# The reciprocals of a bidirectional scan moved from VectorE to ScalarE's Ln and Exp, in a fused attention and FFN kernel

## The chip, the cores and the metric

One core of one Trainium2 chip. The metric is the device time of one launch in microseconds. The kernel before was run three times: 1677.47 us is the median (1675.44 to 1679.04).

## The reference

Four sequences (NB = 4) of 512 positions and 512 channels pass through one block. `f` is a second input of the same shape; both scans use it as their `k` and as their `v`.

```python
# _bi_wkv, per channel; called twice, with other w and u
tf    = sigmoid(sum(time_emb))                      # one number per sequence
decay = exp(-exp(w)) * (0.5 + 0.5 * tf)
ek, ekv = exp(min(k, 30)), exp(min(k, 30)) * v
nf, df = scan(a = a * decay + ekv, b = b * decay + ek)            # forward
nb, db = the same scans from the end
euk = exp(min(u + k, 30))
num = nf + nb - ekv + euk * v
den = df + db - ek + euk
out = sigmoid(r) * (num / max(den, 1e-8)) * (0.8 + 0.2 * tf)

x = x + attention(bi_wkv(x, f, f, w1, u1))   # 16 heads of 128, segments of 128 with a memory (delta rule), then Wo
x = x + ffn(bi_wkv(x, f, f, w2, u2))         # silu(x W1) * (x W3), Walsh-Hadamard transform over 2048, then W2
```

## The kernel before

Everything is written by hand for five queues: `tensor` (TensorE), `vector` (VectorE, DVE in the profile), `scalar` (ScalarE, ACT), `gpsimd` (GpSimd, POOL) and `sync` (SyncE, SP, most DMAs). Each queue runs its instructions in order and waits on semaphores, so an instruction that waits holds up all that stands behind it on its engine. Matrix products are made of three products of split numbers (a high part and what is left): of each weight, ScalarE writes the high part (`split_hi`, L1246, tile `wh`) and GpSimd the rest (`split_w`, L1619, tile `wl`).

**The scans.** The work of `_bi_wkv` is cut into 32 tiles of 128 channels x 512 positions, 16 for each scan. `scan(t, name)` in `vector` writes one step of tile `t`: `df`, `nf` the forward scans (denominator, numerator), `db`, `nb` the backward ones, `mn` and `mu` the minima for the next tile, `d2`, `n2` the sums, `d3` the clamp and the sigmoid of r (L874), `rc0` to `rc3` four reciprocals of 128 columns each (L880), `oy` the output (L885). ScalarE makes the exponentials (`exp_k`, `exp_u`, `exp_r`) and `yh`, GpSimd the products `EKV`, `EUV` and `yl`; `yh` and `yl` are what TensorE needs of a tile.

**The head.** Tiles 0 to 3 come first, with nothing beside them. TensorE's `chunk(c)` makes the first head group's k, v and q from tile `c`: k and v and q take 12 products of 512 columns and 12 of 256. It starts when `yh`, `yl` of tile `c` and the three weights are there. Tiles 0 and 2 use one set of buffers, 1 and 3 another. Behind tile 2, VectorE also makes the mixing weights from `betas` (L1107 to L1111); SP then stores them (`beta_s`), and ScalarE's queue loads them with `load_ombeta(0)`, `load_beta(0)`, which wait for the store and stand ahead of `high_y(3)`.

**The grid.** 32 groups of two heads follow (`n` = 0 to 31). In each, every engine passes eight slots, `behind(n, k)`. A planner, `shared_out()`, deals the steps of tiles 4 to 23, then of the transform of W2 and of z, over the slots: each slot has room in ns (`ROOM`, `BURST_ROOM`), each step a cost in VectorE's time (`SCAN`; 0 for steps of other engines), and the order is that of the table. All engines use the same table, so a step of ScalarE stands in the slot in which its place in the table falls. Where a slot stands on ScalarE: 1 ahead of the copy of the next group's first half of v (`copy_v(nx, 0)`), 4 ahead of the first copy of k, 6 ahead of the first copy of q, 7 behind it and ahead of the second copy of q. Every fourth group is a burst (`n` = 4, 8, ...): TensorE then also does the output projection `wo` and all of k and q at the group's end.

**The FFN.** 32 steps (`u`) follow; tiles 24 to 31 are dealt over them by `shared_out_ffn()`. The first steps wait for weights of the first two hidden blocks, "1", "3" and "2" of blocks 0 and 1.

Of the kernel before, what the change touches and what calls it, by code (L numbers as in the profile page):

```python
# [44 lines left out]
def seg(s):  # L45
# [22 lines left out]
for _i in range(8):  # L68
    for name, cost in HADAMARD:
        if name != "mult":  # L70
            STEPS.append((name, _i, cost))
        elif _i > 0:
            if _i == 2:
                STEPS += [(z, 0, c) for z, c in MODULATE[1:]]
            STEPS.append((name, _i - 1, cost))
            if _i == 1:
                STEPS.append(MODULATE[0][:1] + (0, 0))
STEPS += [("mult", 7, 300)] + [(name, 1, cost) for name, cost in MODULATE]
# [10 lines left out]
def shared_out():  # L89
# [135 lines left out]
def adaln_attn_ffn(nc, xT_d, fT_d, cond_d, wu_d, wq_d, wk_d, wv_d, wo_d, betas_d,  # L225
# [9 lines left out]
    with ExitStack() as ctx:  # L235
# [3 lines left out]
        def sems(names):  # L239
# [80 lines left out]
        sb(ctx, "pad2", [P, NC, T])  # L320
# [29 lines left out]
        a_c, a_bt, a_ek, a_eu, a_er, a_e1, a_yh, a_wh = sems("a_c a_bt a_ek a_eu a_er a_e1 a_yh a_wh")  # L350
# [3 lines left out]
        v_c, v_bt, v_one, v_mn, v_mu, v_nf, v_nb, v_df, v_db, v_ni, v_n2, v_di, v_d2, v_d3, v_rc, v_oy, v_wl = sems(  # L354
            "v_c v_bt v_one v_mn v_mu v_nf v_nb v_df v_db v_ni v_n2 v_di v_d2 v_d3 v_rc v_oy v_wl")
# [443 lines left out]
        def vector(e):  # L799
# [24 lines left out]
            def scan(t, name):  # L824
# [38 lines left out]
                elif name == "d2":  # L863
                    w.wait_ge(v_db, t + 1)
                    w.wait_ge(a_eu, t + 1)
# [11 lines left out]
                elif name[:2] == "rc":  # L877
                    j = int(name[2])
# [1119 lines left out]
```

## Time and profile before

| | |
|---|---|
| median of three runs | 1677.47 us |
| the profiled execution, its device time | 1676.78 us |
| its span, first to last instruction | 1674.8 us |
| TensorE busy | 1579.1 us, 94% |
| VectorE, ScalarE, GpSimd busy | 1160.8, 744.6, 564.2 us |
| granted TensorE clock, mean | 0.986 of full speed |

Device time and span are 2.0 us apart. Busy time of TensorE is modelled from pipelined products: in the tables a product of 512 columns shows some 0.4 us, while the next one starts 0.23 us behind it. In timeline rows the columns are start, duration, engine, line, operation, out<-in with shapes, count, and in brackets the idle time of the engine ahead of the row and what ended it. A row with x4 is four instructions merged.

### The profile page before, as it was taken

Reading aid. Unit: us, or ns where it says so; the run is one execution under the profiler, and the core shown is the slowest. Engines: PE = TensorE matmul, PEld = TensorE weight load, DVE = VectorE, ACT = ScalarE, POOL = GpSimd, SP = SyncE. Lnnn points to the kernel's source line nnn. Section 1 sums busy time; section 2 is a strip of 40 time slices with the busy share of each in tenths; the row PEclk is TensorE's granted clock in tenths of the full one; section 3 lists DMA queues with packets and bytes.
Section 4 is the critical chain, followed back from the end, with each engine's and each line's share of the span. In section 5 each row is a group of like instructions: output and inputs, shape, how many; then the busy total and the mean of one; then the engine's idle time right before and its main releaser. Section 6 shows DMA issues by size and latency. Waiting matters only on the chain.

```text
span 1674.8 us, 26931 instructions
## 1 busy us (share of the span) xinstructions
PE 1579.1 (94%) x9696; PEld 1411.0 (84%) x9696; DVE 1160.8 (69%) x2688; ACT 744.6 (44%) x1623; POOL 564.2 (34%) x406
## 2 busy tenths in 40 slices
PE   0589989999999999999999999999899999999999
PEld 0479988998999999899899899888788888888887
DVE  8778877886887887788775673665887785333333
ACT  3346736544644644553454562652544442222221
POOL 4465656141222212221102010132655453343331
PEclk9789999999999999999999999999999999999999
DMA  3185666549466367446447556347211122321101
GB/s 113 61 310 178 214 207 241 188 151 348 156 212 211 120 208 270 154 171 237 153 163 283 209 214 251 114 169 260 85 63 51 55 79 94 108 62 40 50 14 50
DMA packets 111491, 264.39 MB, mean 158 GB/s; under 512 B 11088, under 2 KB 36096, under 8 KB 110464
## 3 DMA queue, kind: packets, MB, share of 16 engines
q1 hardware_dynamic: 92784, 235.41, 39.8%
q10 hardware_dynamic: 18576, 27.27, 5.3%
q8 instruction: 78, 1.28, 0.3%
q14 instruction: 53, 0.43, 0.1%
HBM read 214.38 MB, written 48.25 MB: 157 GB/s over the span
## 4 chain that ended last, share of the span: by engine, by line
PE 84%; DVE 7%; issue 2%; DMA 2%; ACT 2%; POOL 1%; SPq 1%; ACTq 0%; DVEq 0%; POOLq 0%
PE psG L489 16%; PE psG L491 16%; PE psG L490 16%; PE psX L644 4%; PE psX L489 3%; PE psX L491 3%; PE psX L490 3%; PE psX L597 3%; PE psZ L625 2%; PE psZ L616 2%; PE psZ L624 2%; PE psY L489 2%; PE psY L491 2%; PE psY L490 2%; PE psZ L491 2%
## 5 line engine op out<-in xcount | busy, mean ns | idle before, releaser
L1619 POOL TENSOR_TENSOR wl<-stage,wh 128x512 fp32r<-128x512 f32 x160 | 228.7, 1453 | 179.3 <-ACT wh L1246 178.0
L489 PE MATMUL psG<-yh,wh 128*128 128x512 f32 x632 | 259.1, 410 | 9.4 <-ACT etmp L1387 7.1
L491 PE MATMUL psG<-yh,wl 128*128 128x512 f32 x632 | 248.4, 393 | 0.0
L490 PE MATMUL psG<-yl,wh 128*128 128x512 f32 x632 | 248.4, 393 | 0.0
L1682 POOL TENSOR_TENSOR vs<-v,omb 128x512 f32<-128x512 f32 x64 | 96.3, 1525 | 339.1 <-PE psX L644 333.1
L1689 POOL TENSOR_TENSOR hl<-sg,hh 128x512 fp32r<-128x512 f32 x64 | 86.5, 1351 | 225.1 <-ACT hh L1460 225.0
L489 PE MATMUL psG<-wh,yh 128*128 128x256 f32 x512 | 152.3, 297 | 1.5 <-issue 1.5
L489 PE MATMUL psG<-ah,wh 128*128 128x256 f32 x512 | 146.7, 286 | 2.8 <-POOL wl L1619 1.7
L489 PEld LDWEIGHTS psG<-yh,wh 128*128 128x128 f32 x632 | 120.6, 191 | 30.6 <-issue 7.5
L491 PE MATMUL psG<-wh,yl 128*128 128x256 f32 x512 | 146.0, 285 | 0.0
L490 PE MATMUL psG<-wl,yh 128*128 128x256 f32 x512 | 145.9, 285 | 0.0
L491 PE MATMUL psG<-ah,wl 128*128 128x256 f32 x512 | 144.8, 283 | 0.0
L490 PE MATMUL psG<-al,wh 128*128 128x256 f32 x512 | 144.8, 283 | 0.0
L1246 ACT ACTIVATE wh<-stage 128x512 fp32r<-128x512 f32 x154 | 89.1, 621 | 120.8 <-PE psZ L491 31.3
L491 PEld LDWEIGHTS psG<-yh,wl 128*128 128x128 f32 x632 | 119.8, 190 | 26.1
L490 PEld LDWEIGHTS psG<-yl,wh 128*128 128x128 f32 x632 | 120.6, 191 | 20.1
L1460 ACT ACTIVATE hh<-sg 128x512 fp32r<-128x512 f32 x64 | 40.5, 632 | 171.9 <-DVE sg L1047 171.9
L880 DVE RECIPROCAL DBK<-DF 128x128 f32<-128x128 f32 x120 | 107.8, 928 | 0.6
L1379 ACT ACTIVATE kT<-psG 128x512 f32<-128x512 f32 x62 | 37.0, 596 | 157.9 <-PE psG L491 157.9
L1411 ACT ACTIVATE S<-S,st 128x128 f32<-128x128 f32 x256 | 99.2, 389 | 17.6 <-issue 14.3
L961 DVE CUSTOM_DVE_ANT_0 S<-psX,mask 128x128 f32<-128x128 f32 x256 | 59.5, 287 | 67.2 <-PE psX L597 66.8
L489 PE MATMUL psX<-yh,wh 128*128 128x512 f32 x128 | 52.3, 409 | 53.1 <-POOL wl L1619 45.9
(190 smaller groups left out, 4258.9 us busy)
## 6 DMA issues: line engine op xcount, KB each, us to landing
wh<-high_o SPq DMA_DIRECT2D x52, 512.0 KB, 3.9
wl<-low_o SPq DMA_DIRECT2D x52, 512.0 KB, 5.2
stage<-in_w SPq DMA_DIRECT2D x64, 256.0 KB, 4.0
wh<-high_v SPq DMA_DIRECT2D x24, 512.0 KB, 4.1
wl<-low_v SPq DMA_DIRECT2D x24, 512.0 KB, 5.3
wh<-high_k SPq DMA_DIRECT2D x24, 512.0 KB, 4.2
wl<-low_k SPq DMA_DIRECT2D x24, 512.0 KB, 5.8
wh<-high_q SPq DMA_DIRECT2D x24, 512.0 KB, 4.6
```

What stands on the lines that cost most here:

```text
L489: e.matmul(out, lh, rh, start=first, stop=False, skip_group_check=check)
L490: e.matmul(out, lh, rl, start=False, stop=False, skip_group_check=check)
L491: return e.matmul(out, ll, rh, start=False, stop=last, skip_group_check=check)
L597: m = e.matmul(X[j][:, seg(s)], qT[:, j, seg(s)], kT[:, j, seg(s)], start=True, stop=True)
L644: m = e.matmul(X[j][:, seg(s)], pT[:, j, seg(s)], vs[:, s, j, :], start=True, stop=True)
L880: e.reciprocal(dbk[:, 128 * j:128 * j + 128], df[:, 128 * j:128 * j + 128]).then_inc(v_rc, 1)
L961: m = e.tensor_tensor_reduce(S[:, j, seg(s)], X[j][:, seg(s)], mask[:, :], 1.0, NEG, ALU.add, ALU.max, st[:, 0, j, s:s + 1])
L1246: e.activation(hi, raw, ACT.Copy).then_inc(a_wh, 1)
L1411: m = e.activation(S[:, j, seg(s)], S[:, j, seg(s)], ACT.Exp, bias=st[:, 1, j, s:s + 1], scale=SCALE, accum_out=st[:, 2, j, s:s + 1])
L1619: e.tensor_tensor(lo, raw, hi, ALU.subtract).then_inc(p_wl, 1)
L1682: e.tensor_tensor(vs[:, :, j, :], v[n % 2][:, :, j, 0:P], omb[:, 128 * j:128 * j + 128].rearrange("p (a d) -> p a d", a=1).to_broadcast([P ...
L1689: e.tensor_tensor(hl[u % 2][:, j, :], hid(k)[:, :], hh[u % 2][:, j, :], ALU.subtract).then_inc(p_hl, 1)
```

## The change

The four reciprocals of a tile go. In their place ScalarE makes a first value by `exp(-ln(den))` (`guess`), and VectorE refines it with one Newton step (`e1`, `e2`); the sign it leaves is taken up by `tf`. The order of a tile's steps is new: the denominator's steps first, then ScalarE's `ln`, then the numerator's. The planner's table, three of its rules and the order in the head change with it; the work on `betas` moves behind tile 3. At the end of a burst, splits of later weights move behind the copies of k and q; in the FFN's first step one split moves forward. SP loads the q weights ahead of the 1 MB tile `xb`. Two pads of 32 bytes shift the tiles of the attention stage, and `pad2` makes up for them further on.

```diff
-SCAN = (("df", 1200), ("nf", 1200), ("er", 0), ("di", 80), ("ni", 80), ("db", 1200), ("mn", 420), ("nb", 1200),
-        ("ek", 0), ("d2", 740), ("n2", 740), ("mu", 490), ("ekv", 0), ("d3", 690), ("eu", 0), ("rc0", 900),
-        ("rc1", 900), ("euv", 0), ("rc2", 900), ("rc3", 900), ("oy", 740), ("yh", 0))
+SCAN = (("df", 1200), ("er", 0), ("di", 80), ("db", 1200), ("mn", 420), ("d2", 740), ("ek", 0), ("d3", 690), ("ln", 0),
+        ("nf", 1200), ("ni", 80), ("nb", 1200), ("ekv", 0), ("n2", 740), ("mu", 490), ("eu", 0), ("e1", 690),
+        ("e2", 740), ("euv", 0), ("oy", 740), ("yh", 0))
...
-                if name == "zload" and (n < NN - 1 if i == 1 else n < NN - NG):
+                if name == "zload" and n < (27, 31)[i] or name == "zsig" and (n, k) < ((28, 4), (31, 2))[i]:
...
+        sb(one, "pad5", [P, 8])
         ah = sb(one, "ah", [P, 16, 256], F32R)
         al = sb(one, "al", [P, 16, 256], F32R)
+        sb(one, "pad6", [P, 8])
...
-                elif name[:2] == "rc":
-                    j = int(name[2])
+                elif name == "e1":
+                    w.wait_ge(a_ln, 2 * t + 2)
                     w.wait_ge(v_d3, t + 1)
-                    e.reciprocal(dbk[:, 128 * j:128 * j + 128], df[:, 128 * j:128 * j + 128]).then_inc(v_rc, 1)
+                    e.scalar_tensor_tensor(df, df, 1e38, dbk, ALU.min, ALU.mult).then_inc(v_e1, 1)
+                elif name == "e2":
+                    w.wait_ge(v_e1, t + 1)
+                    e.scalar_tensor_tensor(dbk, df, 2.0, dbk, ALU.subtract, ALU.mult).then_inc(v_e2, 1)
...
-            e.tensor_scalar(tf[:, 2, :], tf[:, 0, :], 0.2, 0.8, ALU.mult, ALU.add).then_inc(v_c, 1)
+            e.tensor_scalar(tf[:, 2, :], tf[:, 0, :], -0.2, -0.8, ALU.mult, ALU.add).then_inc(v_c, 1)
...
+            def tile(t):
+                scan(t, "nf")
+                scan(t, "ni")
+                scan(t, "nb")
+                scan(t, "n2")
+                scan(t, "mu")
+                scan(t, "e1")
+                scan(t, "e2")
+                scan(t, "oy")
+
+            def denominators(t):
+                scan(t, "di")
+                scan(t, "db")
+                scan(t, "mn")
+                scan(t, "d2")
+                scan(t, "d3")
...
+            denominators(0)
+            tile(0)
             scan(1, "df")
...
-            for name in TAIL:
-                scan(0, name)
             scan(2, "df")
...
+            scan(3, "df")
+            denominators(3)
+            tile(3)
             w.wait_ge(a_bt, 1)
             e.tensor_scalar_add(bt, bt, 1.0).then_inc(v_bt, 1)
...
+            def guess(t):
+
+                df, dbk = set_of(t)[1], set_of(t)[3]
+                w.wait_ge(v_d3, t + 1)
+                e.activation(dbk, df, ACT.Ln).then_inc(a_ln, 1)
+                w.wait_ge(a_ln, 2 * t + 1)
+                e.activation(dbk, dbk, ACT.Exp, scale=-1.0).then_inc(a_ln, 1)
...
             exp_u(2)
-            split_hi(1)
-            high_y(0)
             exp_r(2)
             split_hi(2)
+            high_y(1)
             exp_k(3)
             load_k(4)
+            guess(2)
...
                 if burst:
-                    split_hi(here + 13)
                     for j in range(2):
                         copy_kq(nx, "k", j, G[j])
                         exp_kq(nx, "k", j, G[j])
                 if more:
-                    split_hi(here + (14 if burst else 6))
+                    split_hi(here + (12 if burst else 6))
                     copy_kq(nx, "q", 0, G[0])
                     exp_kq(nx, "q", 0, G[0])
+                    split_hi(here + (14 if burst else 6))
...
             split_hi(PLACE["2", 0] + 2)
             sigmoid(1, 1, bank_of(1, 2))
+            split_hi(PLACE["2", 0] + 3)
             behind_ffn(0, 3)
...
-            split_w(PLACE["2", 0] + 2)
+            split_w(PLACE["2", 0] + 3)
             behind_ffn(0, 3)
...
+            load_w(3)
+            e.dma_start(xb[:, :, :], xT_d[0]).then_inc(d_xb[0], 16)
             w.wait_ge(v_bt, 3)
```

VectorE in the head, from tile 0's sums on. `DF`, `NF`, `DBK`, `NBK` are tile 0's buffers, `qT` and `sq` hold tile 1's. Before, the rows from tile 1's numerator scan (backward) on; the last is tile 2's first scan:

```order
L853 SCALAR_TENSOR_TENSOR sq<-dec,last,qT 128x512
L866 SCALAR_TENSOR_TENSOR qT<-sq,gain,kT 128x512
L862 SCALAR_TENSOR_TENSOR qT<-sq,gain,kT 128x512
L821 TENSOR_SCALAR EU<-kx,ucut 128x512
L874 SCALAR_TENSOR_TENSOR DF<-DF,ER 128x512
L880 RECIPROCAL DBK<-DF 128x128 x4
L885 SCALAR_TENSOR_TENSOR OY<-NF,tf,DBK 128x512
L834 SCALAR_TENSOR_TENSOR DF<-dec,EK 128x512
```

In the changed kernel, from tile 0's `d2` on (L861) to tile 1's first scan:

```order
L861 SCALAR_TENSOR_TENSOR DF<-DBK,gain,EU 128x512
L869 SCALAR_TENSOR_TENSOR DF<-DF,ER 128x512
L831 SCALAR_TENSOR_TENSOR NF<-dec,EKV 128x512
L840 TENSOR_SCALAR last<-NF,ends 128x1
L847 SCALAR_TENSOR_TENSOR NBK<-dec,last,NF 128x512
L856 SCALAR_TENSOR_TENSOR NF<-NBK,gain,EUV 128x512
L815 TENSOR_SCALAR kT<-kx,ucut 128x512
L875 SCALAR_TENSOR_TENSOR DF<-DF,DBK 128x512
L878 SCALAR_TENSOR_TENSOR DBK<-DF,DBK 128x512
L883 SCALAR_TENSOR_TENSOR OY<-NF,tf,DBK 128x512
L828 SCALAR_TENSOR_TENSOR qT<-dec,EK 128x512
```

Tile 0's output (`OY`) came behind all of tile 1's scans and now comes ahead of them; the rows between `d3` (L869) and `e1` (L875) stand between ScalarE's call and its use.

ScalarE at the end of group 1, where the next group's q is copied from PSUM (`psG`). Before:

```order
L1379 ACTIVATE qT<-psG 128x512
L1387 ACTIVATE etmp<-psG 128x512
L1390 ACTIVATE etmp<-etmp 128x512
L1264 ACTIVATE ER<-ER 128x512
L1379 ACTIVATE qT<-psG 128x512
L1404 ACTIVATE kn<-psY 128x384 x2
L1387 ACTIVATE etmp<-psG 128x512
L1390 ACTIVATE etmp<-etmp 128x512
```

In the changed kernel:

```order
L1390 ACTIVATE qT<-psG 128x512
L1398 ACTIVATE etmp<-psG 128x512
L1401 ACTIVATE etmp<-etmp 128x512
L1272 ACT_TABLE_LOAD
L1272 ACTIVATE DBK<-DF 128x512
L1274 ACT_TABLE_LOAD
L1274 ACTIVATE DBK<-DBK 128x512
L1283 DMA kx<-in_fT 128x512
L1390 ACTIVATE qT<-psG 128x512
L1415 ACTIVATE kn<-psY 128x384 x2
L1398 ACTIVATE etmp<-psG 128x512
```

Between the two copies of q there stood the Exp of one tile's r (`ER`); now two table loads, the Ln, the Exp and a DMA issue stand there, all of tile 5.

ScalarE at the end of the first burst (`n` = 4). `wh<-stage` is a split, `kT<-psG` a copy of k. Before:

```order
L1246 ACTIVATE wh<-stage 128x512 x4
L1379 ACTIVATE kT<-psG 128x512
L1387 ACTIVATE etmp<-psG 128x512
L1390 ACTIVATE etmp<-etmp 128x512
L1379 ACTIVATE kT<-psG 128x512
L1387 ACTIVATE etmp<-psG 128x512
L1390 ACTIVATE etmp<-etmp 128x512
L1379 ACTIVATE qT<-psG 128x512
L1387 ACTIVATE etmp<-psG 128x512
L1390 ACTIVATE etmp<-etmp 128x512
```

In the changed kernel, from the end of the second copy of k on:

```order
L1401 ACTIVATE etmp<-etmp 128x512
L1245 ACTIVATE wh<-stage 128x512 x2
L1390 ACTIVATE qT<-psG 128x512
L1398 ACTIVATE etmp<-psG 128x512
L1401 ACTIVATE etmp<-etmp 128x512
L1245 ACTIVATE wh<-stage 128x512 x2
L1250 ACTIVATE EK<-EK 128x512
L1272 ACT_TABLE_LOAD
L1272 ACTIVATE DBK<-DF 128x512
L1274 ACT_TABLE_LOAD
L1274 ACTIVATE DBK<-DBK 128x512
L1283 DMA kx<-in_fT 128x512
```

The four splits (x4: the v and k weights of group 6) stood ahead of both copies of k. Now the two of v stand behind them and the two of k behind the first copy of q; tile 8's Ln and Exp with their table loads stand ahead of the second copy of q, which is the next row (not shown).

## Rows read from the trace of the kernel before

**Rows 1.** The page of the profile, its head and part 1.

```profile
span 1674.8 us, 26931 instructions
...
PE 1579.1 (94%) x9696; PEld 1411.0 (84%) x9696; DVE 1160.8 (69%) x2688; ACT 744.6 (44%) x1623; POOL 564.2 (34%) x406
```

**Rows 2.** Busy time by stretch; PEclk is TensorE's granted clock.

```profile
0.00:81.00 81.00, 23.68 (x96) 19.77 (x96) 68.06 (x92) 23.04 (x41) 32.86 (x25) 0.87 0.27 90
...
250.00:262.00 12.00, 6.79 (x21) 5.49 (x22) 5.39 (x6) 6.21 (x12) 8.15 (x7) 0.72 0.90 311
262.00:1170.00 908.00, 898.50 (x6335) 833.42 (x6334) 669.26 (x1878) 451.92 (x1090) 199.38 (x140) 1.00 0.57 202
```

**Rows 3.** TensorE's waits; us in total, times, longest.

```profile
PE psG L489 <- ACT etmp L1387: 7.1, 1, 7.1
```

**Rows 4.** Timeline of VectorE and GpSimd in the head, tiles 0 and 1.

```profile
24.59 1.76 POOL L1625 TENSOR_TENSOR EKV<-EK,kx 128x512 f32<-128x512 f32 x1 [3.57 <-ACT EK L1251]
...
25.20 1.69 DVE L866 SCALAR_TENSOR_TENSOR qT<-sq,gain,kT 128x512 f32<-128x512 f32 x1
...
26.82 0.74 DVE L862 SCALAR_TENSOR_TENSOR qT<-sq,gain,kT 128x512 f32<-128x512 f32 x1
27.87 0.68 DVE L874 SCALAR_TENSOR_TENSOR DF<-DF,ER 128x512 f32<-128x512 f32 x1
28.59 3.39 DVE L880 RECIPROCAL DBK<-DF 128x128 f32<-128x128 f32 x4
```

**Rows 5.** Timeline of TensorE and VectorE, end of the head.

```profile
69.32 0.77 PE L489 MATMUL psX<-yh,wh 128*128 128x512 f32 x1 [7.28 <-POOL yl L1644]
...
71.23 0.75 DVE L885 SCALAR_TENSOR_TENSOR OY<-qT,tf,sq 128x512 f32<-128x512 f32 x1
...
80.17 0.39 PE L491 MATMUL psY<-yh,wl 128*128 128x512 f32 x1
```

**Rows 6.** DMA issues and ScalarE's queue in the head.

```profile
beta_s<-S SPq DMA_DIRECT2D x2, 8.0 KB, 1.4
...
68.07 0.44 ACTq L1284 DMA_DIRECT2D ER<-in_xT  x1
```

**Rows 7.** Timeline of ScalarE, a table load in front of an Exp.

```profile
909.02 1.28 ACT L1390 ACT_TABLE_LOAD   x1
910.32 0.63 ACT L1390 ACTIVATE etmp<-etmp 128x512 f32<-128x512 f32 x1
```

**Rows 8.** Timeline of ScalarE and TensorE around the first burst's end.

```profile
252.88 1.21 ACT L1246 ACTIVATE wh<-stage 128x512 fp32r<-128x512 f32 x2 [7.36 <-DMA stage<-in_wk]
...
255.21 0.76 PE L489 MATMUL psG<-yh,wh 128*128 128x512 f32 x1 [7.11 <-ACT etmp L1387]
```

**Rows 9.** Timeline of ScalarE and TensorE, head group 11.

```profile
457.59 0.57 ACT L1397 ACTIVATE v<-psG 128x512 f32<-128x512 f32 x1
...
459.98 0.40 PE L489 MATMUL psG<-yh,wh 128*128 128x512 f32 x1
...
474.43 0.63 ACT L1390 ACTIVATE etmp<-etmp 128x512 f32<-128x512 f32 x1
476.04 0.60 ACT L1379 ACTIVATE qT<-psG 128x512 f32<-128x512 f32 x1 [0.97 <-PE psG L491]
...
476.49 1.95 PE L597 MATMUL psX<-kT,qT 128*128 128x128 f32 x16
```

**Rows 10.** Timeline of TensorE, two shorter waits, and the stretch behind the first.

```profile
94.41 0.49 PE L624 MATMUL psZ<-mem,sk 128*128 128x129 f32 x2 [2.42 <-DVE mem L975]
...
96.00:98.00 2.00, 2.00 (x11) 2.00 (x11) 2.00 (x7) 0.00 (x0) 1.43 (x1) 0.50 1.04 424
...
222.85 0.35 PE L489 MATMUL psG<-ah,wh 128*128 128x256 f32 x1 [1.71 <-POOL wl L1619]
```

**Rows 11.** Timeline of ScalarE and TensorE, second FFN step.

```profile
1172.24 1.65 ACT L1246 ACTIVATE wh<-stage 128x512 fp32r<-128x512 f32 x3
...
1176.94 0.76 PE L489 MATMUL psX<-yh,wh 128*128 128x512 f32 x1 [6.04 <-POOL wl L1619]
```

More of the change, by code:

```diff
@@ L67 @@
 STEPS += [("hstart", 0, 3000)]
[L68 to L78, printed above, removed]
+STEPS += [(name, i - 1 if name == "mult" else i, cost) for i in range(8)
+          for name, cost in HADAMARD if (name, i) != ("mult", 0)] + [("mult", 7, 300)]
+STEPS += [(name, b, cost) for b in range(2) for name, cost in MODULATE]
 NSLOT = 8
@@ L100, in shared_out @@
                     break
-                if name == "zload" and (n < NN - 1 if i == 1 else n < NN - NG):
+                if name == "zload" and n < (27, 31)[i] or name == "zsig" and (n, k) < ((28, 4), (31, 2))[i]:
                     break
-                if i == 1 and (name == "zsig" and k < 2 or name == "t0" and k < 3):
+                if name == "t0" and i == 1 and k < 3:
                     break
@@ L864, in scan @@
                     w.wait_ge(v_db, t + 1)
+                    w.wait_ge(v_c, 14)
                     w.wait_ge(a_eu, t + 1)
@@ L938, in behind_ffn @@
                         z_late(t, name)
-                    elif name not in ("er", "ek", "ekv", "eu", "euv", "yh", "zload", "zsig", "zh"):
+                    elif name not in ("er", "ek", "ln", "ekv", "eu", "euv", "yh", "zload", "zsig", "zh"):
                         scan(t, name)
@@ L1092, in vector @@
             gains()
-            scan(0, "nf")
-            for name in HEAD:
-                scan(0, name)
+            denominators(0)
+            tile(0)
             scan(1, "df")
-            scan(1, "nf")
-            for name in HEAD:
-                scan(1, name)
-            for name in TAIL:
-                scan(0, name)
-            scan(2, "df")
-            scan(2, "nf")
-            for name in HEAD:
-                scan(2, name)
+            denominators(1)
+            tile(1)
+            scan(2, "df")
+            denominators(2)
+            tile(2)
+            scan(3, "df")
+            denominators(3)
+            tile(3)
             w.wait_ge(a_bt, 1)
@@ L1116, in vector @@
             e.memset(delta[:, :, P:P + 1], 1.0).then_inc(v_one, 1)
-            for name in TAIL:
-                scan(1, name)
-            scan(3, "df")
-            scan(3, "nf")
-            for name in HEAD:
-                scan(3, name)
-            for name in TAIL:
-                scan(2, name)
-            for name in TAIL:
-                scan(3, name)
             for h in range(2):
@@ L1338, in behind @@
                         exp_u(after(i))
-                    elif name == "rc1":
+                    elif name == "ln":
+                        guess(i)
+                    elif name == "e1":
                         load_r(i)
@@ L1361, in behind_ffn @@
                         exp_k(t + 1)
+                    elif name == "ln":
+                        guess(t)
                     elif name == "eu":
@@ L1474, in scalar @@
             load_k(2)
+            guess(0)
             exp_u(1)
             exp_r(1)
+            split_hi(1)
+            high_y(0)
             exp_k(2)
             load_k(3)
+            guess(1)
             exp_u(2)
-            split_hi(1)
-            high_y(0)
             exp_r(2)
             split_hi(2)
+            high_y(1)
             exp_k(3)
             load_k(4)
+            guess(2)
             exp_u(3)
+            exp_r(3)
             split_hi(3)
-            high_y(1)
-            exp_r(3)
+            high_y(2)
             exp_k(4)
             load_k(5)
+            guess(3)
             exp_u(4)
-            high_y(2)
             load_ombeta(0)
@@ L1694, in gpsimd @@
             euv(1)
+            split_w(1)
+            low_y(0)
             ekv(2)
             euv(2)
-            split_w(1)
-            low_y(0)
             split_w(2)
+            low_y(1)
             ekv(3)
@@ L1702, in gpsimd @@
             split_w(3)
-            low_y(1)
+            low_y(2)
             ekv(4)
-            low_y(2)
             euv(4)
```

18 lines of the change are left out of this document (7 added, 11 removed).

## Prediction

> **What bounds the kernel now.** I read the page first, then the busy time by stretch, then TensorE's waits, then the timelines at the places where it waits. TensorE is busy for 1579.1 of 1674.8 us [rows 1]; no other engine comes near. So only time in which TensorE stands counts, and three kinds of it are worth naming. In the first 81 us it works 23.68 us [rows 2]: there VectorE's scans set the pace. Between 250 and 262 us it works 6.79 of 12 us, at 0.72 of its clock [rows 2]: it waits 7.11 us for ScalarE [rows 3, 8], which itself sits 7.36 us before a split whose weights have not landed [rows 8], with the copy that TensorE needs behind it. And at 1176.94 us it waits 6.04 us for the low part of a weight whose high part ScalarE wrote only at 1172.24 [rows 11]. From 262 to 1170 us it works 898.50 of 908 us [rows 2]: there is next to nothing to win there, and every new delay of a copy that TensorE waits for can lose.
>
> **The head.** VectorE makes the four tiles back to back: the first reciprocals start at 28.59, the last output at 71.23 [rows 4, 5]. Four reciprocals take 3.39 us [rows 4]. `e1` and `e2` have the form of `d3` and `n2`, 0.68 and 0.74 us [rows 4]; with the step from one dependent instruction to the next, 0.72 each (27.87 to 28.59), so 1.44. A tile saves 3.42 - 1.44 = 2.0 us, four tiles 8.0 us. Two things are taken off. First, GpSimd: its product at 24.59 lasts 1.76 us, and VectorE's sum that starts at 25.20 takes 1.69 us, where its twin at 26.82 takes 0.74 [rows 4]: VectorE stands for some 0.95 us while GpSimd reads. The reciprocals ran through such operations untouched (3.39 us for four of 0.85). In the head GpSimd has 19 operations, of which about 14 hit VectorE now (counted in the timeline; five fall on reciprocals). With the reciprocals gone nearly all will: 3 to 4 more, 3.3 us. Second, the work on `betas` (2.4 us) stood ahead of tile 3 and now stands behind it, which brings the last output forward by as much. Sum: output of tile 3 at 71.23 - 8.0 + 3.3 - 2.4 = 64.1, its end at 64.9; since the scans now also stand bare against GpSimd at the new places, I take 66.
>
> But `high_y(3)` stands behind two loads on ScalarE's queue that wait for the stored betas. These are now made after the output: 1.4 us for the three small operations, 0.4 for the second issue, 1.4 to land [rows 6], then three DMA issues of 0.34 to 0.45 us (the last of them in [rows 6]), 1.3 in sum: `yh` starts at 66 + 4.5, and `yl`, 1.9 later, is there at 72.4. Were it not held, it would be there at 66 + 1.9. TensorE has drained its other chunks by about 67 and is cold: before, chunk 2 started cold at 69.32 behind 7.28 us of idleness, and two chunks ended at 80.57 [rows 5], 6.9 us cold and 4.3 warm. So the last chunk ends at 72.6 + 6.9 = 79.5. **Head: -1.1 us, with the copies behind it -1.5** (bounds -4 and +2: GpSimd's hits none or all; if `yh` were not held the gain would be 5.6). The covering of ScalarE's latency: from `d3` to the end of Exp I take 0.63 + 1.30 + 0.63 and the semaphores, 2.7 us; VectorE has `nf`, `ni`, `nb`, `n2`, `mu` in between, 3.6 us and more. `e1` does not wait. Without that cover each tile would wait up to 2.7 us.
>
> **What a guess costs ScalarE.** Ln and Exp are not in the set that is loaded: the changed order has two table loads for each tile. A load takes 1.28 us, and the Exp behind it starts 1.30 after it, for 0.63 us [rows 7]. Ln isn't in the trace; the nearest row is that Exp, and every 128x512 operation of ScalarE takes 0.6 to 0.7 us. So 1.30 + 0.54 + 1.30 + 0.63 = 3.8 us, 20 times in the grid. The first load runs ahead of the wait for `d3`, so a late `d3` costs little. The Trainium skill (ScalarE: Activation LUTs, What ACT_TABLE_LOAD costs) puts a switch at 1.28 us and 1.38 us of drain, 2.66 in all. The trace has no such drain; by the page a guess would take some 6.5 us.
>
> **Where it meets TensorE.** I take a plain group, 11, as the scale. The copy of v starts at 457.59 and TensorE goes on into that bank at 459.98: 1.8 us of slack behind the copy's 0.57 [rows 9]. The copy of the second half of q starts at 476.04, done at 476.64; TensorE's scores start at 476.49 and need it half way, at 477.4: 0.75 us of slack [rows 9]. A guess of 3.8 us thus costs: in slot 1, ahead of `copy_v`, 3.8 - 1.8 = 2.0 us; with the tile's `ek` (0.5) in it 2.6. In slot 7, it starts when the Exp of q ends at 475.06 [rows 9] and the copy ends at 479.5: 2.1 us, with the DMA issue 2.3. In slot 6 it starts at about 471.4, 1.9 us of ScalarE's idle time are used up, and the copy is late by 0.3, with `ek` by 0.8. In slots 2 to 5 the next copies have 2 to 5 us: 0 to 0.5. In slot 0 it pushes the softmax and then `copy_v`: 1.2. From the tables the guesses fall: group 1 slot 7 (2.3); 5 slot 6 (0.8); 7 slot 1 (2.6); 9 slot 0 (1.2); 20 slot 1 (2.1); and the other 14 (without group 4's last) with 0.2 on the mean (2.4 with rounding of bursts). Sum 11.4 us. A wait of over 2 us also costs clock: behind the 2.42 us of idleness that end at 94.41, TensorE goes at 0.50 of its clock, 1.2 GHz; behind the 1.71 us at 222.85 its products stay at 0.28 us, full clock [rows 10]. A cool stretch of 4 us costs 2 us of work; the three waits of 2.1 to 2.6 us are at that border: +1.5. **Guesses in the grid: +12.9 us** (bounds: +3, if VectorE's and ScalarE's new leads hide all but the longest; +20, if all cool).
>
> **The burst.** With the splits behind the copies, ScalarE copies k when it is there, and 7.11 us go, and 2.1 us of work lost to the cold clock (about 4.2 us at half clock; the mean of 0.72 over these 12 us [rows 2] stands for 3.4 lost, the rest of it while idle). But tile 8's guess falls in slot 7 of this group: the split of k waits for its load until 252.9 as now, ends at 254.1, `ek` 254.6, guess 258.5, copy 259.2; TensorE, now early, wants it at 255.4. It waits 3.8 to 4.2 us and cools again: +6.3. **-2.9 us** (bounds -9.2 and 0).
>
> **The FFN's start.** The split moves from 1172.24 [rows 11] to behind `sigmoid(1, 1)`, near 1165, GpSimd's part ends near 1169, before TensorE asks at 1170.9. So 6.04 us go and 2.05 of clock. In return tile 24's steps, now ahead of the last addition to `xb`, hold that by 0.5 us, and the first gate of step 2, due 1185.6, comes about 1 us late behind three table loads. **-6.6 us** (bounds -8.1 and -3). Later steps have over 10 us of slack for each bank, and TensorE is full there. The pads and the order of SP's first loads I cost at nothing: the q weights are split at 54 us, long after they land; without that cover they'd cost a landing, some 3 us.
>
> Sum on the profiled 1676.78: -1.5 + 12.9 - 2.9 - 6.6 = +1.9, 1678.7; the median of three lies 0.7 above the profiled one. I take 1678.
>
> **Rivals.** A: as summed, the repairs and the new holds cancel: 1678 (1671 to 1686), chance 0.42. B: the copies have more slack than group 11 shows, because VectorE has 2 us less work a tile and the calls come early; the grid then loses 3 instead of 12.9 and the burst's second wait shrinks to 1, so it wins 8.2: 1676.8 - 1.5 + 3 - 8.2 - 7 = 1663 (1657 to 1671), 0.33. For it: ScalarE is busy 44% only [rows 1]. Against: the slack that counts is the copy's deadline, not busy time. C, slower: each call ahead of a copy in slots 0, 1, 6 and 7 cools TensorE, +2 us each at nine places more than I have counted, 1678 + 18 = 1696 (1686 to 1704), 0.17. It decides if waits down to 1 us are followed by half clock; the 1.71 us at 222.85 speak against it [rows 10]. D: each table load holds ScalarE for longer than the trace shows, by one more load's 1.28 us; 2.6 us more a call, where it is due, at thirteen places: 1678 + 34 = 1712, 0.03. This is what the drain that the page of the Trainium skill named above adds would do; the 1.30 us from load to Exp speak against it [rows 7]. E: the betas are not late, and the head gains 5.6 instead of 1.5: 1674, with B's grid lower still: 0.05, from 1666 to 1676.
>
> **Numbers.** A measurement of this kernel can tell a change of about 0.2% (3.4 us) from none: the borders are 1674.1 and 1680.9. A's 0.42 falls as faster 0.06, same 0.21, slower 0.15; B's 0.33 and E's 0.05 as faster 0.35, same 0.03; C and D are slower, 0.20. Together: faster 0.41, same 0.24, slower 0.35. The range from 1661 to 1692 takes in A, most of B and E and the lower half of C; A's own is 1671 to 1686.
>
> **What would show it.** Right: VectorE's head without reciprocals, last output near 66, `yh` 4.5 us behind it; no wait at 255 but one of about 4 us some 4 us later; no wait at 1177; waits of about 2 us for v's or q's copy in groups 1, 7 and 20; ScalarE's busy time up by 28 x 3.8 plus the head's 15, to some 850 us; VectorE's down by 32 x 2.0. Wrong: a table load with a gap behind it, an `e1` that waits for ScalarE (its first instruction then shows "<-ACT"), or grid groups as long as before, 26.25 us each.

## The result and the profile after

The changed kernel takes 1721.59 us (median of 4 runs, 1718.78 to 1722.16) against 1677.18 before: ratio 1.0261, 95% interval 1.0245 to 1.0276. It is 44 us slower; forecast was no change, 1678, with 1692 as the upper end. The profile's page, head and part 1:

```profile
span 1719.5 us, 27047 instructions
...
PE 1592.3 (93%) x9696; PEld 1412.7 (82%) x9696; DVE 1112.7 (65%) x2624; ACT 861.7 (50%) x1751; POOL 557.6 (32%) x406
```

VectorE lost 48 us of work and ScalarE gained 117 [rows 1]. TensorE's busy time rose by 13 us for the same products: some ran on a lower clock. The stretches of [rows 2], and four short ones behind waits:

```profile
0.00:81.00 81.00, 23.76 (x97) 19.70 (x98) 65.43 (x84) 39.09 (x58) 34.33 (x25) 0.87 0.27 90
152.00:156.00 4.00, 3.84 (x23) 3.87 (x24) 2.60 (x12) 3.29 (x8) 0.00 (x0) 0.66 0.82 266
250.00:262.00 12.00, 12.00 (x60) 10.02 (x59) 10.19 (x19) 6.91 (x13) 7.02 (x7) 1.00 0.69 251
264.00:268.00 4.00, 0.76 (x3) 0.79 (x4) 3.93 (x8) 3.96 (x8) 3.92 (x4) 0.74 0.90 334
268.00:272.00 4.00, 4.00 (x21) 4.00 (x20) 3.25 (x16) 2.22 (x4) 3.92 (x4) 0.50 1.00 371
424.00:428.00 4.00, 3.92 (x12) 3.26 (x13) 0.00 (x0) 0.55 (x2) 0.00 (x0) 0.50 0.87 299
```

The 12 us at 250 are full now, where 5.2 were idle. The wait of [rows 3] is gone; the 1.0 us that is left between the same two (`psG` and `etmp`) is another one, at 541.82. The loss is elsewhere, and TensorE's waits name the places:

```profile
PE psX L483 <- DVE sg L1039: 12.6, 9, 2.8
...
PE psG L483 <- ACT v L1408: 6.4, 3, 3.3
PE psG L483 <- DMA wl<-low_q: 6.0, 1, 6.0
...
PE psX L591 <- issue: 5.5, 2, 3.5
PE psG L483 <- DVE sg L1039: 4.7, 5, 2.3
```

`v` and the two "issue" waits (scores, L591, whose q copy is late) are the grid; `sg` is the FFN: TensorE wants a bank of PSUM that VectorE's gate has not emptied, because ScalarE's sigmoid ahead of the gate is late.

To see where time goes, I use three landmarks in ScalarE's timeline: the first copy of v (before: 90.15 us, end of the head), the first `hh<-sg` (before: 1121.34, where the FFN starts), and the span's end. Differences to before, us:

| | head | grid, to the FFN's start | FFN | span |
|---|---|---|---|---|
| changed kernel | -0.2 | +25.8 | +19.1 | +44.7 |

**Where the calls stand.** End of group 1: two table loads, Ln, Exp, and only then the second copy of q. ScalarE, and TensorE's scores behind it:

```profile
147.71 1.28 ACT L1272 ACT_TABLE_LOAD   x1
149.00 0.63 ACT L1272 ACTIVATE DBK<-DF 128x512 f32<-128x512 f32 x1
149.65 1.28 ACT L1274 ACT_TABLE_LOAD   x1
149.73 0.35 ACTq L1283 DMA_DIRECT2D kx<-in_fT  x1
150.94 0.63 ACT L1274 ACTIVATE DBK<-DBK 128x512 f32<-128x512 f32 x1
151.48 0.58 ACT L1390 ACTIVATE qT<-psG 128x512 f32<-128x512 f32 x1
```

```profile
152.16 0.57 PE L591 MATMUL psX<-kT,qT 128*128 128x128 f32 x3 [1.97 <-issue]
```

The call lasts 3.86 us (147.71 to 151.57; 3.8 had been taken), with no gap behind a load. The wait of 1.97 us is followed by 0.66 of the clock at 152 to 156. The first burst has the wait that was forecast, some 8 us later than forecast: Ln at 264.09, Exp at 266.03, the copy at 266.57, and the scores start at 267.24 behind 3.54 us of idleness, at half clock to 272.

**The FFN.** ScalarE between the two sigmoids of a step, and the bank that TensorE waits for:

```profile
1232.30 0.63 ACT L1471 ACTIVATE hh<-sg 128x512 fp32r<-128x512 f32 x1 [1.55 <-DVE sg L1044]
1232.95 1.28 ACT L1272 ACT_TABLE_LOAD   x1
1234.25 0.63 ACT L1272 ACTIVATE DBK<-DF 128x512 f32<-128x512 f32 x1
1234.90 1.28 ACT L1274 ACT_TABLE_LOAD   x1
...
1236.19 0.63 ACT L1274 ACTIVATE DBK<-DBK 128x512 f32<-128x512 f32 x1
1236.84 1.28 ACT L1463 ACT_TABLE_LOAD   x1
1238.13 0.60 ACT L1463 ACTIVATE sg<-psG 128x512 f32<-128x512 f32 x1
```

```profile
1239.51 0.50 PE L483 MATMUL psG<-yh,wh 128*128 128x512 f32 x1 [1.28 <-DVE sg L1039]
```

Here a call has three loads ahead of the sigmoid, since the sigmoid's table must come back: 5.2 us from 1232.95 to the sigmoid. The sigmoid's own loads are not more than before (12, where there were 13, since the tiles' Exp made them necessary already); what is new is two loads for each of 32 calls, 94 in all against 30.

### The profile page after: what moved, and what is told of

It reads as the page before. It is cut to its first block, busy times and chain, and to the rows that moved or that the text cites. A ratio compares the mean times of both kernels' runs of the same rounds, so it can differ in the third digit from the quotient of the medians.

```text
span 1719.5 us, 27047 instructions
## 1 busy us (share of the span) xinstructions
PE 1592.3 (93%) x9696; PEld 1412.7 (82%) x9696; DVE 1112.7 (65%) x2624; ACT 861.7 (50%) x1751; POOL 557.6 (32%) x406
## 3 DMA queue, kind: packets, MB, share of 16 engines
q8 instruction: 78, 1.28, 0.3%
## 4 chain that ended last, share of the span: by engine, by line
PE 66%; DVE 14%; ACT 8%; issue 6%; DMA 3%; SPq 1%; POOL 1%; ACTq 1%; DVEq 0%; POOLq 0%
PE psG L483 13%; PE psG L485 12%; PE psG L484 12%; PE psX L591 3%; PE psX L638 3%; PE psZ L619 2%; PE psX L483 2%; PE psX L485 2%; PE psX L484 2%; PE psZ L610 2%; PE psZ L618 2%; PE psY L628 1%; PE psY L647 1%; PE psY L579 1%; ACT wh L1245 1%
## 5 line engine op out<-in xcount | busy, mean ns | idle before, releaser
L1635 POOL TENSOR_TENSOR wl<-stage,wh 128x512 fp32r<-128x512 f32 x160 | 223.3, 1420 | 196.7 <-ACT wh L1245 195.1
L485 PEld LDWEIGHTS psG<-yh,wl 128*128 128x128 f32 x632 | 119.8, 190 | 27.2
L1422 ACT ACTIVATE S<-S,st 128x128 f32<-128x128 f32 x256 | 99.2, 389 | 12.3 <-issue 11.9
L483 PEld LDWEIGHTS psG<-ah,wh 128*128 128x128 f32 x512 | 96.9, 189 | 8.8 <-issue 7.7
```

Of the source, the lines that this page charges most:

```text
L483: e.matmul(out, lh, rh, start=first, stop=False, skip_group_check=check)
L485: return e.matmul(out, ll, rh, start=False, stop=last, skip_group_check=check)
L1422: m = e.activation(S[:, j, seg(s)], S[:, j, seg(s)], ACT.Exp, bias=st[:, 1, j, s:s + 1], scale=SCALE, accum_out=st[:, 2, j, s:s + 1])
L1635: e.tensor_tensor(lo, raw, hi, ALU.subtract).then_inc(p_wl, 1)
```

## The experiments

Each median is of 4 to 10 runs; the kernel before gave 1676.9 to 1679.4 beside them, so differences of medians between groups of runs are good to some 3 us, and the ratio in brackets, to the kernel before beside them, is the safer number.

**Reciprocals back in one stage (e1, e2) or everywhere (e3).** `RC` is the range of tiles whose `e1`, `e2` and call are replaced by `rc0` to `rc3`, at 900 ns each in the table, in the new order of steps; it is 24 to 31, 4 to 23 and 0 to 31.

```diff
+                elif name[:2] == "rc":
...
+                    m = e.reciprocal(dbk[:, 128 * j:128 * j + 128], df[:, 128 * j:128 * j + 128])
...
             def guess(t):
+                if t in RC:
+                    return
```

> The changed kernel with four reciprocals on VectorE again for tiles 24 to 31, in the new order of steps; the head and the grid keep the calls of ScalarE. Theory L (ScalarE's own time for a call, Ln, Exp and their table loads, stands ahead of the FFN's sigmoids, whose gates free TensorE's banks): the 25.6 us that the FFN loses from its third step on go, 1721.6 - 25.6 = 1696. Rival O (the new order of a tile's steps and the planner's new places make VectorE's gates late, whoever makes the reciprocal): 1720 to 1724, since the reciprocals cost VectorE 2 us a tile more.

> The changed kernel with reciprocals for tiles 4 to 23 alone, in the new order; head and FFN keep the calls. Theory L: the grid's 25.3 us go and the burst's wait at 267 too, so that the repair of the first burst shows whole: 1721.6 - 25.3 - 9 = 1687. Rival O: at most the four waits right behind a call (1.97, 3.54, 1.34, 3.34 us with their low clock) go, some 16 us: 1705 or more.

> All 32 tiles with reciprocals, everything else of the change kept (denominators first, the splits moved, q weights ahead of xb, pads). Theory L: before's 1677.2 less the first burst's 9 and the FFN's start of 6.3, with a head 1 to 2 us longer than the changed one: 1663. Rival O: the new order costs by itself, 1680 or more.

Measured: 1696.83 (ratio 1.0112), 1695.89 (1.0109) and 1675.72 (0.9992, 0.9981 to 1.0003). What replaces the reciprocal costs 25 us in the FFN, the number of theory L, and 26 in the grid, where L had 34. But these runs do not part L from O: with 3600 ns of reciprocals in the table a tile also takes up its old room again, so both the call and the closer packing of the tiles go. Run e13 below shows that L's number was met by luck: with the calls kept and only the old packing restored, the FFN wins nearly as much. With reciprocals everywhere L had 1663, and it is 1675.7: some 12 us are missing. Part of them is the first burst's repair, of which little stays (e7 below); the rest goes to rival O.

**Calls without table loads (e4).**

```diff
-                e.activation(dbk, df, ACT.Ln).then_inc(a_ln, 1)
+                e.activation(dbk, df, ACT.Copy, scale=0.0).then_inc(a_ln, 1)
-                e.activation(dbk, dbk, ACT.Exp, scale=-1.0).then_inc(a_ln, 1)
+                e.activation(dbk, dbk, ACT.Copy).then_inc(a_ln, 1)
```

> The changed kernel with ScalarE's Ln and Exp of each call replaced by two copies (the first scaled by zero), for which no table is loaded; places, waits and VectorE's steps are the changed kernel's, and the tiles' outputs are zero. Theory L in the form that the table loads are what costs (2.6 of 3.8 us a call, and a reload for the next sigmoid in the FFN): nearly all goes, 1675 or less. Rival Q (what costs is that ScalarE's queue stands for VectorE's clamp, or the call's place ahead of a copy): the waits stay, 1705 or more.

Measured: 1697.27 (1.0114). The loads cost 24.3 us, a good half of the loss of 44. Neither theory is right alone: 20 us stay, though ScalarE hardly waits for the clamp in the changed kernel (three times in 28 calls, 2.9 us at the most).

**The old pace (e5).** The table's costs decide how many steps fall into a slot. Dropping 3600 ns of reciprocals for 1430 ns made a tile 2170 ns shorter in the table, and the tiles follow each other faster.

```diff
-        ("nf", 1200), ("ni", 80), ("nb", 1200), ("ekv", 0), ("n2", 740), ("mu", 490), ("eu", 0), ("e1", 690),
-        ("e2", 740), ("euv", 0), ("oy", 740), ("yh", 0))
+        ("nf", 1200), ("ni", 80), ("nb", 1200), ("ekv", 0), ("n2", 740), ("mu", 490), ("eu", 0), ("e1", 1775),
+        ("e2", 1825), ("euv", 0), ("oy", 740), ("yh", 0))
```

> The changed kernel with e1 and e2 put into the planner's table at 1775 and 1825 ns instead of 690 and 740, so that a tile takes up as much room as before and the tiles follow each other at the old pace (16 FFN steps for the last eight instead of 14, later groups in the grid). No instruction is taken away. Theory P (the calls hurt because the shorter tiles of the new table are packed more closely, so that more of ScalarE's work falls into each group and step): half of the 50 us comes back, 1697 or less. Theory L (a call costs what it does wherever it stands): 1715 to 1722.

Measured: 1690.88 (1.0071, 1.0053 to 1.0089). 30.7 us come back by two numbers in a table: theory P. (The changed table deals the last eight tiles over 13 FFN steps, not 14; the old pace takes 16. With the pace each call also moves to another slot, so "packing" below means both.)

**No call at all, close packing (e6).**

```diff
-                    w.wait_ge(a_ln, 2 * t + 2)
...
-                    e.scalar_tensor_tensor(df, df, 1e38, dbk, ALU.min, ALU.mult).then_inc(v_e1, 1)
+                    e.scalar_tensor_tensor(df, df, 0.0, dbk, ALU.min, ALU.mult).then_inc(v_e1, 1)
...
             def guess(t):
...
+                return
```

> The changed kernel without ScalarE's Ln and Exp and their table loads; VectorE keeps e1 and e2 with changed operands, so that the outputs of the tiles are zero, and nothing waits for ScalarE. It bounds what VectorE's saving of 2 us a tile could bring if the call were free. If VectorE's time counts beyond the head: below the 1675.7 of the kernel with reciprocals everywhere, by 5 us for the head and by more for the grid, 1665 or less. If it counts in the head alone: 1670. If the new order with its closer tiles costs by itself: 1680 or more.

Measured: 1696.79 (1.0102). The third case: the new order with its closer tiles costs by itself. It also equals e4 within 0.5 us (ratios 1.0102 and 1.0114): ScalarE's two operations without their loads cost nothing that can be told. One place in e6 shows what is overfull. GpSimd and VectorE ahead of the first `mem` of group 5, and TensorE:

```profile
268.47 1.78 POOL L1637 TENSOR_TENSOR EKV<-EK,kx 128x512 f32<-128x512 f32 x1
269.05 1.75 DVE L874 SCALAR_TENSOR_TENSOR DF<-DF,DBK 128x512 f32<-128x512 f32 x1
270.72 1.27 DVE L1012 TENSOR_TENSOR al<-psY,ah 128x512 fp32r<-128x512 f32 x2
271.92 0.68 DVE L1023 SCALAR_TENSOR_TENSOR sq<-qT,etmp 128x512 f32<-128x512 f32 x1
272.52 1.75 DVE L877 SCALAR_TENSOR_TENSOR DBK<-DF,DBK 128x512 f32<-128x512 f32 x1
274.30 1.63 DVE L882 SCALAR_TENSOR_TENSOR OY<-NF,tf,DBK 128x512 f32<-128x512 f32 x1
275.86 0.48 DVE L971 TENSOR_TENSOR mem<-psZ,mem 128x129 f32<-128x129 f32 x2
```

```profile
276.19 0.58 PE L618 MATMUL psZ<-mem,sk 128*128 128x129 f32 x1 [8.12 <-DVE mem L971]
```

`e1`, `e2` and `oy` have 690, 740 and 740 ns in the table and take 1.75, 1.75 and 1.63 us here, beside operations of GpSimd. Not all of the 8.12 us is packing: the same wait is 6.16 us in e4 and 4.14 at the old pace (e9, the next run).

**The old pace, no table loads (e9).** e5 with e4's copies.

> The kernel e5 (old pace) with its two ScalarE operations of a call replaced by copies that need no table load, the first scaled by zero, so the outputs of the tiles are zero. It splits the 15 us by which e5 (1690.9) is slower than reciprocals everywhere (1675.7). If the table loads are what a call costs: 1672 to 1677. If the two operations themselves, or e1 and e2 under GpSimd's locks, cost as well: 1682 or more.

Measured: 1676.33 (0.9994, 0.9985 to 1.0003). With e4, e5 and the changed kernel it makes a square:

| | with table loads | without |
|---|---|---|
| close packing | 1721.6 | 1697.3 |
| old pace | 1690.9 | 1676.3 |

The packing costs 21.0 us without loads and 30.7 with them; the loads cost 14.6 at the old pace and 24.3 packed. Each makes the other dearer by 9.7. By the ratios it is 11.7; the four intervals together leave either number open by some 5 us.

**The FFN's pace alone (e13).** As e5, in `FSTEPS` only.

```diff
-FSTEPS = [(name, t, cost) for t in range(NA, NT) for name, cost in SCAN + LATE]
+FSCAN = tuple((name, {"e1": 1775, "e2": 1825}.get(name, cost)) for name, cost in SCAN)
+FSTEPS = [(name, t, cost) for t in range(NA, NT) for name, cost in FSCAN + LATE]
```

> The changed kernel with e1 and e2 at 1775 and 1825 ns in the table of the FFN alone (tiles 24 to 31 take 16 steps again, not 14); the grid stays packed closely. Nothing else is changed. If the FFN's loss is its own packing and the calls at the old pace cost little there (e5's FFN ran 4.9 us faster than before's, the changed one's 18.8 slower): 1721.6 - 24 = 1698. If the FFN's loss comes from what the grid hands on: 1715 or more.

Measured: 1699.70 (1.0132). The FFN's loss is its own packing, and at the old pace the eight calls cost it nothing that shows: -4.4 us against before with them (e13), -4.6 without their loads (e9, table below).

**VectorE lighter, still packed (e14).** e6 without `e1` and `e2`; the output is multiplied by zero.

```diff
                 elif name == "e1":
...
+                    return
+                elif name == "e2":
+                    return
...
-                    e.scalar_tensor_tensor(oy_of(t)[:, :], nf, tf[:, 2, b:b + 1], dbk,
+                    e.scalar_tensor_tensor(oy_of(t)[:, :], nf, 0.0, dbk,
```

> The kernel e6 (no call, close packing) with VectorE's e1 and e2 left out too; the output takes a factor of zero. VectorE has 1.44 us less a tile than in e6, everything else falls into the same slots. If the closer packing costs because VectorE's slots are overfull (e1 and e2 last 0.85 to 0.9 us in the grid, not 0.69 and 0.74): 1682 or less. If it costs through the other engines' and queues' work per step: 1692 or more.

Measured: 1680.10 (1.0016, 1.0003 to 1.0028), 16.7 less than e6. The bar of 1682 was badly set: the two steps are also missing in the head, which is 8.4 us shorter. By the landmarks (table below) the grid loses 7.9 us to before instead of 14.6, the FFN 3.2 instead of 5.5. So VectorE's overfull slots are a part of what the packing costs. How large a part stays open: e15, with e6's grid, lost 10.1 there, so the 6.7 us of the grid may be as few as 2.2.

**SyncE's loads of z one step later (e15).** e6, in the FFN.

```diff
                 for k in range(4):
-                    behind_ffn(u, k)
+                    if u > 1:
+                        behind_ffn(u - 1, k)
```

> The kernel e6 with SyncE's loads of z in the FFN issued one step later, behind the weights' loads of that step. In e6 a load of z waits for VectorE's zl until 1296.8 us, the weights behind it land at 1301.3 and ScalarE's splits stand ahead of the sigmoid that TensorE waits for. If this queue is what the closer packing costs in the FFN: its 11.7 us go in part, 1690 or less. If not: 1695 to 1698.

Measured: 1688.26 (1.0066), 8.5 less than e6, 6.0 by the ratios. What it takes away stands in e6's rows. SyncE, which waited for `zl` until here, then loads the weights behind:

```profile
1296.84 0.33 SPq L1921 DMA_DIRECT2D ZS<-x_s  x1
1297.27 3.14 SPq L1794 DMA_DIRECT2D stage<-in_w  x4
```

ScalarE splits them ahead of a sigmoid, and TensorE waits for the gate:

```profile
1301.32 1.31 ACT L1244 ACTIVATE wh<-stage 128x512 fp32r<-128x512 f32 x2 [5.54 <-DMA stage<-in_w]
1303.74 1.16 ACT L1244 ACTIVATE wh<-stage 128x512 fp32r<-128x512 f32 x2 [1.11 <-DMA stage<-in_w]
1304.81 0.58 ACT L1459 ACTIVATE sg<-psX 128x512 f32<-128x512 f32 x1
```

```profile
1306.17 0.50 PE L483 MATMUL psX<-yh,wh 128*128 128x512 f32 x1 [2.25 <-DVE sg L1038]
```

**The splits alone, on the kernel before (e7 both, e8 the FFN's only).**

```diff
-                    split_hi(here + 13)
...
-                    split_hi(here + (14 if burst else 6))
+                    split_hi(here + (12 if burst else 6))
                     copy_kq(nx, "q", 0, G[0])
                     exp_kq(nx, "q", 0, G[0])
+                    split_hi(here + (14 if burst else 6))
...
             sigmoid(1, 1, bank_of(1, 2))
+            split_hi(PLACE["2", 0] + 3)
...
-            split_w(PLACE["2", 0] + 2)
+            split_w(PLACE["2", 0] + 3)
```

> The kernel before with nothing but the two moves of splits (at the bursts' ends and in the FFN's first step). If the repairs stay whole: 7.1 us of waiting and 2.1 of clock at the first burst, 6.0 and 2.0 at the FFN's start, 1677.5 - 17 = 1661. If the first burst's part is given back by later waits, as 4 to 5 of 9 us were between groups 5 and 10 in the run with reciprocals everywhere: 1666.

> The kernel before with the FFN's split alone moved forward (ScalarE's and GpSimd's part of one weight). Step of the prediction: -8.1 without the table loads of a call beside it, 1669.5. Rival: what comes early here waits later in the FFN, 1675 or more.

Measured: 1666.49 (0.9922, 0.9907 to 0.9938) and 1669.42 (0.9937, 0.9921 to 0.9953). The FFN's move holds what it promised; the bursts' is worth 2.9 us instead of 9, and since the intervals of the two runs overlap, even that is not told from none. It is given back at later waits of TensorE in e7, of which these two are the longest; the second was 2.34 us before:

```profile
263.44 0.49 PE L624 MATMUL psZ<-mem,sk 128*128 128x129 f32 x2 [3.68 <-DVE mem L975]
...
384.49 0.79 PE L489 MATMUL psG<-yh,wh 128*128 128x512 f32 x1 [3.52 <-DMA wl<-low_q]
```

ScalarE's sixth pair of v copies starts at 260.72 instead of 270.76, 10.0 us early (2.0 of it from ahead of the burst); the tenth pair is only 3.5 early.

**The mixing weights (e10), and what is worth keeping (e11, e12).** e10 is the changed kernel with

```diff
-            load_ombeta(0)
-            load_beta(0)
-            load_r(3)
             high_y(3)
+            load_ombeta(0)
+            load_beta(0)
+            load_r(3)
```

e11 has calls in the head alone, and the table, rules and reciprocals of before from tile 4 on; e12 is e11 with this edit.

> The changed kernel with the two loads of the mixing weights behind high_y(3) on ScalarE's queue instead of ahead of it. The prediction says that yh of tile 3 is held 4.5 us by them. If so, TensorE's wait of 5.74 us at 73.8 us shrinks to about 1 and the start of the grid moves: 1721.6 - 5 = 1716.5. Rival: the next thing behind (GpSimd's yl, the splits) holds it anyway: 1720.

> The changed kernel's head (calls for tiles 0 to 3) and its three repairs (splits at the bursts and in the FFN, SP's order, pads), but the planner's table and rules of before and four reciprocals from tile 4 on. The head of the changed kernel ended level with before, so this should equal e7: 1666.5 (1664 to 1668). If the new head, the pads or SP's order cost or bring something that the head's end doesn't show: off by over 3 us.

> The kernel of e11 with the loads of the mixing weights behind high_y(3). If both findings add: 1666.5 - 5 = 1661.5, 0.990 of before. If the wait of 5.74 us is only handed on: 1666.

Measured: 1718.20 (1.0252), 1668.19 (0.9945, 0.9931 to 0.9959) and 1662.67 (0.9921, 0.9907 to 0.9934, five runs). The wait of 5.74 us is cut in both edited kernels, to 2.03 in e10 and 2.17 in e12, and the head ends 2.5 us earlier than the changed kernel's in e10, 3.9 earlier than e11's in e12. In e12 `yh` starts at 67.15, behind the output of 65.46. e11 ends 1.7 us above e7 (3.9 by the ratios), so the new head, the pads and SP's order together bring nothing that shows. e12 has the lowest median of the study, 14 us under before; by ratio it is level with e7, which has no call anywhere.

**The landmarks of all of them**, from their profiled executions, us against before:

| | head | grid | FFN |
|---|---|---|---|
| changed kernel | -0.2 | +25.8 | +19.1 |
| e1 reciprocals in the FFN | -0.1 | +25.5 | -5.9 |
| e2 reciprocals in the grid | -0.1 | +0.6 | +18.3 |
| e3 reciprocals everywhere | +2.3 | +0.7 | -5.3 |
| e4 no loads | +0.6 | +11.9 | +8.7 |
| e5 old pace | +0.4 | +17.8 | -4.8 |
| e6 no call | +0.7 | +14.6 | +5.5 |
| e9 old pace, no loads | +0.6 | +3.2 | -4.6 |
| e13 FFN at the old pace | +0.4 | +27.2 | -4.4 |
| e14 no e1, e2 | -7.7 | +7.9 | +3.2 |
| e15 z later | +2.6 | +10.1 | -0.9 |
| e7 splits alone | -0.5 | -2.7 | -6.6 |
| e8 the FFN's split alone | -1.4 | -1.5 | -6.0 |
| e10 late loads of the weights | -2.7 | +24.2 | +18.5 |
| e11 calls in the head alone | +1.3 | -4.8 | -5.6 |
| e12 | -2.6 | -4.8 | -3.9 |

These are single executions, and a few us of a difference are chance: e15's grid has e6's program and ends 4.5 us better, e12's FFN has e7's and is 2.7 worse.

The square, taken apart by stage: in the grid the loads cost 13.9 us packed (25.8 - 11.9) and 14.6 at the old pace (17.8 - 3.2), the packing 8.0 and 8.7. In the FFN the loads cost 10.4 packed and nothing at the old pace, the packing 23.9 with loads and 13.3 without. So, as far as single executions tell, loads and packing simply add up in the grid, and what each makes the other dearer lies in the FFN.

## Why the prediction was wrong

**The head: right.** Its last output was forecast for 66 and starts at 65.43; `yh` starts at 71.68 (70.5 forecast), behind the loads of the mixing weights. TensorE goes on at 73.79 (72.6). The head gains 0.2 us, not 1.5. That `yh` is held by these loads is shown by the rows of e10 and e12. In time it gives 5.5 us by e12 against e11 (4.0 by the ratios, and the intervals overlap a little); e10's 3.4 us are within the noise of two measurements (ratios 1.0252 and 1.0261).

**A call's length: right.** 3.86 us for 3.8; ScalarE's busy time rose to 861.7; the forecast said 850, but its own terms (744.6 + 28 x 3.8 + 15) make 866. VectorE's fell by 48 us, not by 32 x 2.0 = 64: the reciprocals took 114.6 and `e1` and `e2` take 53.2, which saves 61, and its other steps take 13 us longer. There is no gap behind a load (149.65 + 1.28 = 150.93, the Exp starts at 150.94), so the drain that the Trainium skill (ScalarE: Activation LUTs, What ACT_TABLE_LOAD costs) adds is not seen in this kernel either.

**"Guesses in the grid: +12.9" and "the burst: -2.9": the sum missed a term, and one term was given back.** From the end of the head on the grid loses 25.8 us, forecast 10.0 (19.2 for the calls, less 9.2 for the burst's repair). The calls were not underrated: 13.9 by e4 or 11.2 by e6, against the 12.9 and 6.3 that I had put on them. The waits forecast behind them are there: 1.97 us in group 1 (2.3 forecast), 1.34 in group 7 (2.6), 3.34 in group 9 (1.2) and 1.77 in group 20 (2.1). The other 11.9 us are there without a load. I read the new table for where calls fall, and never asked what it costs that tile 17 now ends in group 13 instead of 16. This term, the packing, is 8.7 us of it (11.9 - 3.2, e4 against e9). The last 3.2 (e9) stand where the forecast had -9.2 for the repair: the repair doesn't last (next paragraph), and some 6 us between e9's +3.2 and e7's -2.7 stay unexplained. A part of the packing is VectorE (e14): the prediction had counted GpSimd's hits on the new steps in the head (3 to 4 more) and not in the grid, where `e1` and `e2` last 0.88 and 0.85 us on the mean:

```profile
L875 DVE SCALAR_TENSOR_TENSOR DF<-DF,DBK 128x512 f32<-128x512 f32 x20 | 17.6, 882 | 0.0
L878 DVE SCALAR_TENSOR_TENSOR DBK<-DF,DBK 128x512 f32<-128x512 f32 x20 | 16.9, 847 | 0.3
```

These are groups of VectorE's instructions between 107 and 1150 us (busy, mean ns). The reciprocals they replace had 900 in the table and took 930 on the mean (80 between the same times in the profile of before, 72.4 us busy).

**The burst's repair: right at its place, then given back.** The 12 us at 250 are full, as forecast, and the wait of about 4 us that follows is there with 3.54 and half clock behind it, at 267 and not near 259. That the rest stays was wrong: e7 keeps about 3 of 9.2 us.

**The FFN's start: right.** Forecast -6.6; without calls e7 gains 6.6 in the FFN and e8 6.0 (span -8.9, of which -2.9 ahead of the FFN), and no wait for a `wl` is left there, nor in the changed kernel.

**"Later steps have over 10 us of slack for each bank": the step that failed worst.** I read it from TensorE's side, from one use of a bank to the next. Between them lie ScalarE's queue (a sigmoid, two copies of h, splits, EK, EU, all waiting in order for VectorE or a DMA) and now up to three table loads, and the slack was used up by both: at 1288.72 TensorE waits 2.83 us because ScalarE itself stood 5.48 us for weights, at 1214.58 it waits 2.79 because ScalarE worked all but 0.27 us from 1201.29 to the end of the sigmoid at 1213.80, four table loads of 1.28 us among it. The FFN's body loses 19.1 + 6.6 = 25.7 us, priced at nothing. Without a call the packing alone takes 5.5 + 6.6 = 12.1 of it (e6), and e15 shows that about half of these (6.4 by the landmarks, 6.0 by the ratios) are SyncE's load of z standing ahead of the weights. The loads take 10.4 more while the steps are packed (e4) and nothing at the old pace.

Rival B (0.33) fell with the grid, which loses 25.8 us and not 3. Rival C had the sign but not the mechanism: waits of about 1 us (1.34 at 335.83, 0.96 at 143.80) had full clock behind them. It gave 1696. Nor does the prediction's "a wait of over 2 us also costs clock" hold as it stands. Behind 1.97 us at 152.16 the clock fell to half, but behind 2.06 and 2.27 us in the FFN it stayed whole, so the length of the wait alone does not decide it. The wait of 2.27 us, and the 4 us behind it (the last numbers are the granted clock, 1.00, and the DMA share and rate):

```profile
1369.58 0.50 PE L483 MATMUL psG<-yh,wh 128*128 128x512 f32 x1 [2.27 <-DVE sg L1039]
```

```profile
1369.00:1373.00 4.00, 3.42 (x15) 2.83 (x16) 3.86 (x7) 1.92 (x2) 1.94 (x2) 1.00 0.00 0
```

The rule of D (a drain) would have come nearest with 1712, for a reason that the rows exclude.

**Still open:** how the packing's price in the grid divides. Three waits of TensorE are longer packed (e4) than at the old pace (e9), without loads in either: for `low_q` at group 8 6.28 us against 3.21 (2.34 before), for `mem` at group 5 6.16 against 4.14, for `wl` near 225 3.53 against 1.84; together 6.8 of 8.7 us, but none was tried alone. And why e3 gains only 1 to 3 us, not told from none, though it has both repairs. Its profile has waits of 2.44 and 1.69 us at 1097 to 1103, at the end of group 30, that e7's has not; e5 and e9 have the like (1.98 and 3.01, 2.46 and 3.02), and these three have the changed rules for z's steps, e7 those of before. This was not tried alone.

## What to carry to other kernels

Where a table of costs deals work over slots, a cost is also a pace: when an operation gets cheaper on one engine, the steps of all the others move closer together, and the dealt work must be priced again on every queue. Two numbers in the table were worth 31 us here, more than the table loads. Move work to another engine only where that engine's queue has nothing behind it that the bound engine waits for: in the head the calls did no harm, in the FFN none at the old pace, but in the grid they cost 14 us at either pace, ahead of copies that TensorE waits for. And follow a repaired wait to the next resource that the engine then meets early.

## What the runs showed of the hardware

Two 128x512 operations of ScalarE for each of 32 tiles cost nothing that can be told as long as no table is loaded (e4 against e6, 1697.3 and 1696.8), while the loads, 1.28 us each and 64 more of them than before, cost 24.3 in the packed table and 14.6 at the old pace. `scalar_tensor_tensor` of 128x512 takes 0.69 us in the head and, where GpSimd works beside it, 1.75; reciprocals of 128x128 hardly change (on the mean 0.91 in the head, 0.93 in the grid). Waits of TensorE of 1.71, 2.06 and 2.27 us left its clock whole; waits of 1.97, 2.42 and 3.54 us had half clock behind them.
